# A fused convolution, state-space scan and expert layer: B read from SBUF instead of PSUM, one slot product on GpSimd, and another order at the end of the period

## The reference

```python
x = x + conv(_gn(x))                       # group norm, graph mixing of 64 nodes
t = tokens(x)
t = t + attn(_ln_t(t))                     # the scan below
t = t + ffn(_ln_t(t))                      # 8 experts, top 2 of them, gelu
```

```python
x_conv = silu(x_main @ W_conv + b_conv)
B_proj, C_proj = split(x_conv @ W_bc + b_bc)
dt = softplus(x_conv @ W_dt + b_dt)
h  = exp(dt_t[..., None] * A) * h + dt_t[..., None] * B_t[:, None, :] * x_t[..., None]
y_t = (h * C_t[:, None, :]).sum(-1)
y  = y * silu(x_gate)                      # then @ W_out + b_out
```

## Time and profile before

| what | us |
|---|---|
| three timed runs, median | 446.93 |
| lowest and highest of them | 444.72 and 447.65 |
| the profiled execution, its own time | 440.92 |
| its span in the profile | 439.2 |
| busy in the span: PE, DVE, ACT, POOL | 377.5, 338.7, 279.2, 247.9 |

### The profile page before, as it was taken

One profiled execution on the slowest core, in us unless ns is written; L12 is line 12 of the kernel. 1 busy time (PEld: TensorE's weight loads), 2 busy tenths in 40 slices (PEclk: granted clock), 3 DMA queues, 4 the chain that ended last, 5 costly groups with the idle time before them and its releaser, 6 DMA issues.

```text
span 439.2 us, 5613 instructions
## 1 busy us (share of the span) xinstructions
PE 377.5 (86%) x1785; PEld 207.6 (47%) x1785; DVE 338.7 (77%) x452; ACT 279.2 (64%) x450; POOL 247.9 (56%) x260
## 2 busy tenths in 40 slices
PE   0786779755699989998999899989988998998995
PEld 0673437212455346534653465355535544553652
DVE  3788347986499679987997799779987997996411
ACT  1002657843577887796779677986877785672472
POOL 9334004764259555875586558655873686387032
PEclk9997988969599999998999899999998999899999
DMA  8570079899999966997598769876988697000000
GB/s 211 163 146 1 0 175 222 222 227 221 226 217 219 225 167 150 228 208 175 137 223 198 175 143 226 187 175 151 220 185 203 141 225 164 1 1 0 13 0 12
DMA packets 22388, 67.91 MB, mean 155 GB/s; under 512 B 5052, under 2 KB 13400, under 8 KB 15448
## 3 DMA queue, kind: packets, MB, share of 16 engines
q1 hardware_dynamic: 21192, 66.73, 66.6%
q10 hardware_dynamic: 1168, 0.84, 0.8%
HBM read 62.32 MB, written 5.24 MB: 154 GB/s over the span
## 4 chain that ended last, share of the span: by engine, by line
PE 59%; DVE 16%; issue 7%; DMA 6%; ACT 5%; POOL 4%; SPq 0%; POOLq 0%; DVEq 0%; ACTq 0%
PE P L1119 11%; PE P L1105 7%; PE P L1135 6%; PE P L1059 5%; DMA av<-dt_scratch 5%; PE P L1106 5%; DVE hs L711 4%; PE P L991 4%; DVE P L704 4%; POOL hs L342 3%; PE P L1093 2%; PE P L1153 2%; PE P L1009 2%; PE P L1016 1%; PE P L1076 1%
## 5 line engine op out<-in xcount | busy, mean ns | idle before, releaser
L342 POOL TENSOR_TENSOR hs<-hs,Cs 128x1024 f32<-128x1024 f32 x64 | 151.7, 2371 | 83.5 <-DVE hs L711 83.5
L711 DVE TENSOR_TENSOR_SCAN hs<-av,P 128x1024 f32<-128x1024 f32 x64 | 146.3, 2287 | 3.2 <-DVE P L704 1.0
L704 DVE SCALAR_TENSOR_TENSOR P<-P,bbcol,ub 128x1024 f32<-128x1024 f32 x62 | 79.8, 1287 | 15.2 <-PE P L1026 12.2
L583 ACT ACTIVATE hb<-P,b1c 128x512 f32<-128x512 f32 x128 | 80.9, 684 | 16.0 <-PE P L1106 13.2
L545 ACT ACTIVATE av<-av,Aneg 128x510 f32<-128x510 f32 x92 | 61.1, 712 | 13.8 <-DMA av<-dt_scratch 13.8
L1119 PE MATMUL P<-hb,W2s 128*64 128x256 f32 x512 | 68.7, 391 | 0.0
L1105 PE MATMUL P<-X,W1H 128*128 128x512 f32 x128 | 56.1, 438 | 6.1 <-ACT av L545 6.1
L1135 PE MATMUL P<-W1H 128*128 128x512 f32 x164 | 56.0, 468 | 0.5 <-DVE rt L762 0.5
L1106 PE MATMUL P<-X,W1L 128*128 128x512 f32 x128 | 50.4, 394 | 0.0
L354 POOL TENSOR_TENSOR accs<-accs,mes 128x256 f32<-128x256 f32 x56 | 40.9, 731 | 12.2 <-DVE mes L796 7.3
L1119 PEld LDWEIGHTS P<-hb,W2s 128*64 128x64 f32 x512 | 31.3, 136 | 31.8 <-issue 22.1
(11 more groups left out here) (188 smaller groups left out, 483.1 us busy)
## 6 DMA issues: line engine op xcount, KB each, us to landing
ub<-u_scratch SPq DMA_DIRECT2D x31, 1024.0 KB, 11.6
av<-dt_scratch SPq DMA_DIRECT2D x23, 1024.0 KB, 7.4
dt_scratch<-dts SPq DMA_DIRECT2D x7, 256.0 KB, 2.8
u_scratch<-rl SPq DMA_DIRECT2D x7, 256.0 KB, 2.8
av<-in_L_conv_Wr SPq DMA_DIRECT2D x2, 576.0 KB, 6.6
av<-in_L_conv_Wl SPq DMA_DIRECT2D x2, 576.0 KB, 7.3
res<-in_x SPq DMA_DIRECT2D x4, 256.0 KB, 4.8
hb<-in_L_ffn_W SPq DMA_DIRECT2D x2, 512.0 KB, 5.5
```

The lines of the kernel that those rows point to most:

```text
L342: gp.tensor_tensor(hs[:, at, :, :], hs[:, at, :, :], rep(Cs[:, p, :], 1, 2), ALU.mult).then_inc(S["cm"], 1)
L583: a_.activation(hb[:, r % 4, :], P[:, (XA, XB)[r % 2], :], ACT.Gelu, bias=b1c[:, r:r + 1]).then_inc(S["gl"], 1)
L704: v.scalar_tensor_tensor(out=ring, in0=rep(P[:, BB, :], 1, 2), scalar=bbcol[:, 0:1], in1=ub[:, 2 * n:2 * n + 2, :], op0=ALU.add, op1=ALU.m ...
L711: v.tensor_tensor_scan(hs[:, (SLOTS * g + n) % RING].rearrange("p a t -> p (a t)"), av[:, 2 * n:2 * n + 2, :].rearrange("p a t -> p (a t)" ...
```

## The change

**B in SBUF.** ScalarE copies B from bank BB, with its bias, to a new buffer `Bs` of two halves (`act_b`), behind the first pair of gelus (in step 0 behind the last exponential). The product on VectorE becomes a tensor_tensor of `ub` and `Bs`, both in SBUF, still into `ring`; it waits for `bs` instead of `b_mm`. B's matmul stands before the first pair instead of at the end of the period.

**One product on GpSimd.** The product of slot 2 (POOLED) is made by GpSimd in place, ub = ub * Bs (`pool_product`), behind slot 1 and the low part; the scan of slot 2 reads `av` and `ub`, both in SBUF.

**The low part.** L754 leaves VectorE; GpSimd makes it (`pool_x2`) behind slot 1.

**The order.** The router's bias is added by VectorE (a new small tensor_tensor, `lgb`) instead of by TensorE, and its logits go to bank XC instead of YS. The spreads of dt for blocks 12 to 15 alternate between YS and XA. On TensorE the four sums stand together behind dt's projection; cenA and varA of step i+2 move between the spreads; the transpose of the router's weights stands behind pair 0 instead of pair 1, and what follows it is one pair earlier; the warming matmuls of a steady period go from 20 to 7. ScalarE follows with a new EXP_ORDER.

```diff
-EXP_ORDER = (0, 1, 2, 3, 4, 5, 6, 7, 8, 12, 9, 10, 13, 11, 14, 15)
+EXP_ORDER = (0, 1, 2, 3, 4, 5, 6, 7, 8, 9, 10, 12, 13, 11, 14, 15)
...
+        Bs = sb("Bs", [128, 2, T])
+        POOLED = 2
...
+        def pool_product(eng, g, p):
+
+            n = POOLED
+            eng.wait_ge(S["bs"], g + 1)
+            eng.wait_ge(S[f"u_in{n // 2}"], 16 * (g + 1))
+            at = ub[:, 2 * n:2 * n + 2, :]
+            gp.tensor_tensor(at, at, rep(Bs[:, p, :], 1, 2), ALU.mult).then_inc(S["pbm"], 1)
+
+        def pool_x2(eng, g):
+
+            eng.wait_ge(S["xh2"], g + 1)
+            eng.wait_ge(S["cm"], min(SLOTS * (g + 1) + 2, SLOTS * G))
+            since(eng, "acc", EXP * g)
+            gp.tensor_tensor(X2[64:128, :], xnt2[:, :], X2[0:64, :], ALU.subtract).then_inc(S["xl2"], 1)
+
         def pool_router(eng, g):
 
+            eng.wait_ge(S["xl2"], g + 1)
...
                 pool_slot(eng, i, p, 1)
+                if prev is not None:
+                    pool_x2(eng, prev)
+                    eng.wait_ge(S["xl2"], prev + 1)
+                pool_product(eng, i, p)
                 if prev is not None:
                     pool_router(eng, prev)
...
+        def act_b(eng, g, p):
+
+            eng.wait_ge(S["b_mm"], g + 1)
+            since(eng, "scan", SLOTS * (g - 1))
+            a_.activation(Bs[:, p, :], P[:, BB, :], ACT.Identity, bias=bbcol[:, 0:1]).then_inc(S["bs"], 1)
...
+            if n == POOLED:
+                eng.wait_ge(S["pbm"], g + 1)
+                src = ub[:, 2 * n:2 * n + 2, :]
             else:
...
-                v.scalar_tensor_tensor(out=ring, in0=rep(P[:, BB, :], 1, 2), scalar=bbcol[:, 0:1], in1=ub[:, 2 * n:2 * n + 2, :],
-                                       op0=ALU.add, op1=ALU.mult).then_inc(S["bm"], 1)
...
+                v.tensor_tensor(ring, u_of, rep(Bs[:, g % 2, :], 1, 2), ALU.mult).then_inc(S["bm"], 1)
...
-                                 ring.rearrange("p a t -> p (a t)"), 0.0, ALU.mult, ALU.add).then_inc(S["scan"], 1)
+                                 src.rearrange("p a t -> p (a t)"), 0.0, ALU.mult, ALU.add).then_inc(S["scan"], 1)
```

More of the change, by code:

```diff
@@ L627, in body @@
                     act_c(eng, nxt, q)
-                act_decay(eng, i, 9, 10, 13)
+                act_decay(eng, i, 12)
+                if nxt2 is not None:
+                    act_lnA1(eng, nxt2)
+                act_decay(eng, i, 13, 11)
+                if nxt2 is not None:
+                    act_lnA2(eng, nxt2)
                 if prev is not None:
                     act_router(eng, prev)
-                act_decay(eng, i, 11, 14, 15)
+                act_decay(eng, i, 14, 15)
+                if prev is None:
+                    act_b(eng, nxt, q)
                 if prev is not None:
@@ L635, in body @@
                         act_gelu(eng, prev, n)
-                        if n == 1:
+                        if n == 0 and nxt is not None:
+                            act_b(eng, nxt, q)
+                        if n == 0:
                             act_wt(eng, prev)
-                        if n in range(2, 6):
-                            act_wb(eng, prev, n - 2)
+                        if n in range(1, 5):
+                            act_wb(eng, prev, n - 1)
                 if nxt2 is not None:
@@ L661, in _ @@
             act_c(eng, 0, 0)
-            eng.wait_ge(S["b_mm"], 1)
-            a_.activation(B0, P[:, BB, :], ACT.Identity, bias=bbcol[:, 0:1]).then_inc(S["b0"], 1)
+            act_b(eng, 0, 0)
             act_lnA1(eng, 1)
@@ L682, in _ @@
                 act_gelu(eng, G - 1, n)
-                if n == 1:
+                if n == 0:
                     act_wt(eng, G - 1)
-                if n in range(2, 6):
-                    act_wb(eng, G - 1, n - 2)
+                if n in range(1, 5):
+                    act_wb(eng, G - 1, n - 1)
         ring = P[:, 0:2, :]
@@ L932, in body @@
                     dve_xn(eng, 1)
+                elif nxt is not None:
+                    dve_relu(eng, nxt)
                 if prev is not None:
                     dve_gate(eng, prev)
-                if i > 0 and nxt is not None:
-                    dve_relu(eng, nxt)
-                if prev is not None:
                     dve_t1(eng, prev, q)
@@ L1296, in body @@
                     pe_pair(eng, prev, 8)
-                pe_sum(eng, i, 0)
-                pe_sum(eng, i, 1)
                 if nxt2 is not None:
                     pe_dtz(eng, nxt2)
-                if nxt is not None:
-                    pe_b(eng, nxt)
-                pe_sum(eng, i, 2)
-                if i + 3 < G:
-                    pe_cenA(eng, i + 3)
-                if prev is not None:
-                    pe_warm(eng, 4, XB)
-                pe_sum(eng, i, 3)
+                for k in range(4):
+                    pe_sum(eng, i, k)
             for i in range(G):
@@ L1323, in _ @@
             pe_router(eng, G - 1)
-            eng.wait_ge(S["dd"], G)
             pe_warm(eng, 8)
             pe_pair(eng, G - 1, 0)
+            pe_wt(eng, G - 1)
             pe_warm(eng, 4)
-            pe_pair(eng, G - 1, 1)
-            pe_wt(eng, G - 1)
-            for n in range(2, 6):
+            for n in range(1, 5):
                 pe_pair(eng, G - 1, n)
-                pe_wb(eng, G - 1, n - 2)
-            for n in range(6, 9):
+                pe_wb(eng, G - 1, n - 1)
+            for n in range(5, 9):
                 pe_pair(eng, G - 1, n)
```

123 lines of the change are left out of this document (59 added, 64 removed).

## The result

The changed kernel takes 502.25 us in the median of 4 runs (497.95 to 506.07), the kernel before 445.83 beside it (444.19 to 447.65). The ratio is 1.123, with a 95% interval of 1.112 to 1.134: slower by 12%. I had predicted 498, in a range of 438 to 515. The profiled execution has a span of 502.6 against 439.2, so 63.4 are to be found.

A forecast was written before the change was run, and what follows sets the result against it. VectorE and TensorE were taken to share the bound. Under blocking, +48 for six periods, -1 for the last step, +8 at the start and 0 after the last scan gave +55 on 440.92, so 496; predicted 498, range 438 to 515.

The forecast's parts named there:

- The likeliest case: VectorE's two-SBUF-input instructions and GpSimd's SBUF reads block each other for whole instructions: 498 us likeliest, 465 to 515, chance 0.70.
- The price of blocking: VectorE's products beside GpSimd: each delayed between 0 and a whole GpSimd multiplication, 2.37 us; the blocking price was taken.
- two heaps: Product durations at L737: 1.2 us where GpSimd is idle, 2.5 to 3.0 where GpSimd began first.
- The period: Steady period under blocking, scan end to scan end: +7.1 to 50.8 us; six periods 305 instead of 256.7.
- 3 to 4: Slot 4: GpSimd, late from the router, multiplies slot 2 until 5.3 after scan 2; scan to scan 5.05 instead of 3.72.
- 4 to 5: Slot 5: the product waits behind GpSimd's multiplication after the experts; scan to scan 5.95 us instead of 4.28.
- The start: Up to slot 7 of step 1: +8 us; step 0 mostly hidden behind loads, step 1 has +8.5.
- the rule I gave for slot 3: Slot 3: with nothing between on VectorE, the product starts ahead of GpSimd; scan to scan 3.75 against 3.65.
- After the last scan: Tail of the kernel: GpSimd and VectorE hardly meet, so 0 us added.
- B's wait: Before slot 0's product: the 2.88 us wait per period for TensorE's B goes, turned into a wait for the port.
- no blocking: Rival, chance 0.22: VectorE's tensor_tensor runs freely beside GpSimd; 1.4 to 1.5 less for six periods, -9, 432 us.
- VectorE goes first: Variant of blocking: where GpSimd is behind, the product starts first, costing GpSimd 1.2, not VectorE 1.7; 454 to 475 us.

The follow-up runs named there:

- the one in which GpSimd is punctual: The changed kernel with slot 2's product back on VectorE, B still in SBUF: 518.51 us, ratio 1.166.

## Why the prediction was right, and where its sizes were off

The likeliest case (blocking, chance 0.70) came true, and the time lies 4 above the forecast. Step by step:

*The price of blocking.* Between 0 and a whole GpSimd multiplication I took the hold. Three runs stand behind it: 1,287 to 2,343 ns by B's place alone, back to 1,287 with B in PSUM, and 1,277 with fills on GpSimd. That L704's successor would fall into two heaps, 1.2 and 2.5 to 3.0, is half right: 26 of 54 lie there, 22 between 1.6 and 2.4, where only the end of a GpSimd instruction or a shorter one is in the way, and 6 reach 3.3 to 3.41, because a product that starts right behind GpSimd's start waits for all of it.

*The period.* Predicted 50.8 from scan end to scan end; the period to which the timelines above belong takes 50.35, from the end of slot 0's scan at 265.02 to the next at 315.37. Slot by slot, measured against predicted: 0 to 1, 7.07 and 7.25; 1 to 2, 10.62 and 10.95; 2 to 3, 3.78 and 3.75; 3 to 4, 4.09 and 5.05; 4 to 5, 7.20 and 5.95; then 5.86, 5.85 and 5.88 and each time 5.95. Two are off, and both come from what I overlooked at slot 2. I had counted the router's small steps only as victims on VectorE, never asked what the new scan does to GpSimd's. It holds L375 for 1.93. Hence the weights are late, TensorE idles and comes back at 1.2 GHz, and the experts let VectorE wait 2.48 (4 to 5 is longer). The other, 3 to 4, is shorter because I had GpSimd too late: its multiplication of slot 2 was to last until 5.3 after scan 2, but it starts at 284.81 and ends 4.46 after it, so slot 4's product waits only about 0.5. That the period is so near the forecast is in part luck, as -0.96 and +1.25 nearly cancel. The six steady periods take 297.6 (159.90 to 457.50) against 256.70: +40.9, where I had +47 for them (48, and 1 off for the last step). They are not all alike: in some, slot 1 takes 5.94 instead of 7.07, because the product starts 0.01 ahead of GpSimd's dts (317.76 and 317.77) and is free (1.22).

*The start.* I added 8 up to slot 7 of step 1; it is +15.4, 159.90 against 144.5. I had step 0 hidden behind its loads and +8.5 in step 1. It is the other way round: the end of slot 0's scan of step 1 comes at 115.67 against 100.27, already +15.4, and step 1 adds nothing, since the kernel before has a wait of its own there (18.5 from slot 1 to slot 2, against 10.9 after). VectorE's timeline of the changed kernel in step 0:

```profile
78.37 2.29 DVE L743 TENSOR_TENSOR_SCAN hs<-av,ub 128x1024 f32<-128x1024 f32 x1 [7.98 <-POOL ub L362]
...
92.46 3.41 DVE L737 TENSOR_TENSOR P<-ub,Bs 128x1024 f32<-128x1024 f32 x1
95.90 2.29 DVE L743 TENSOR_TENSOR_SCAN hs<-av,P 128x1024 f32<-128x1024 f32 x1
98.32 3.37 DVE L737 TENSOR_TENSOR P<-ub,Bs 128x1024 f32<-128x1024 f32 x1
```

and GpSimd's:

```profile
92.40 2.37 POOL L342 TENSOR_TENSOR hs<-hs,Cs 128x1024 f32<-128x1024 f32 x1 [3.49 <-DVE hs L743]
```

Of slot 3 I had written "here the product starts first, as VectorE has nothing between". Even with nothing between it is a matter of hundredths: GpSimd starts at 92.40, the product (here slot 5's) at 92.46, and all the products of slots 3 to 7 in step 0 take 3.3 to 3.4. In step 0 no slot has experts behind it, so the rule I gave for slot 3 would have made all of them free. That step failed. In the steady periods slot 3 came out as forecast (3.78 and 3.75), but because GpSimd is still in its router steps.

*After the last scan.* I had 0; it is 45.1 against 38.0, +7. Stretches of the changed kernel there:

```profile
457.50:470.00 12.50, 9.20 (x34) 5.88 (x35) 2.48 (x6) 1.84 (x5) 3.76 (x3) 0.73 0.04 10
470.00:476.00 6.00, 2.93 (x12) 1.77 (x10) 4.10 (x17) 2.78 (x4) 2.37 (x6) 0.89 0.02 3
476.00:482.00 6.00, 5.87 (x19) 3.61 (x20) 0.00 (x0) 1.75 (x3) 0.08 (x1) 0.54 0.00 0
482.00:502.60 20.60, 15.37 (x88) 8.51 (x87) 3.50 (x8) 9.98 (x16) 5.84 (x8) 0.99 0.03 7
```

TensorE is granted 0.73, 0.89 and 0.54 up to 482, and 0.99 over the rest; before, the whole stretch from 401.20 has 0.99. In the prediction's sum this is the term put at 0. The low part on GpSimd, 1.26 instead of 0.69, is on the path there too. Which of the two weighs more I didn't test.

*The gains.* B's wait went, as forecast, and was worth nothing: even with B in PSUM, taking most of it away brought 0. My rival "no blocking" with -9 had the right sign for the rest of the change: its order and the low part alone, with B in PSUM, gave -1.2%. Its other half, a product less for VectorE, costs 35 with B in PSUM. The rival "VectorE goes first" is there in part: some products of slot 1 start ahead of dts, and slot 3's, behind a router step of 0.25, holds L380. That such an order keeps the changed kernel 16 below the one in which GpSimd is punctual is my reading of the two timelines; no run shows it apart.

*The sum.* +15.4, +40.9 and +7.1 are the 63.4 of the two spans. The +55 predicted fell 8 short: 7 too little in the start, 6 too much in the periods, 7 too little in the tail.

## What to carry to other kernels

Before a VectorE operand is moved from PSUM to SBUF beside a busy GpSimd, count the SBUF inputs: with one of two in PSUM the products and scans ran beside GpSimd here without a loss, with both in SBUF each engine stood still behind the other for up to whole instructions, and the smallest instruction paid the most for its size. Two inputs are not the only case: VectorE's cast of 64x512, with one SBUF input, takes 0.42 free and in the kernel with B in PSUM 1.58 in the median, ending 0.29 behind GpSimd's multiplication (259.69 against 259.40). Where this can't be avoided, look not at the busy time but at what stands behind the held instruction: with B in PSUM a 32-column router step held by a scan cost 15 us, because TensorE waited for it, and a wait added on purpose won it back. And try the parts of a change apart, each on the base that will remain: the order was worth 0.8% by itself, the product on GpSimd was worth 16 with B in SBUF and cost 35 with B in PSUM.

## What the runs showed of the hardware that I had not expected

- Who starts first decides who pays, and hangs on hundredths. Both engines are released by the same scan end; GpSimd went first by 0.05 to 0.06 at 288.66 and 92.40. With B in SBUF alone the product of slot 3 started at 269.58, 0.04 ahead of GpSimd's 269.62; it took 1.23 and GpSimd's multiplication 3.42. The profile does not show what makes the product start 0.03 after a scan in one case and 0.12 in the other.
- A scan holds like any other VectorE instruction with two SBUF inputs: 0.24 became 2.16 on GpSimd. With one input in PSUM its 2,286 ns did not change, whatever GpSimd did. The scan can be held too: with slot 2's product of the kernel before written into ub, the scan of step 0 took 3.26 behind GpSimd's rl (L329), and the multiplication by C that came behind the scan 4.33.
- GpSimd's fills of the same tile, 0.95 to 0.97 for 1,024 columns, held nothing: the product took 1,277.
- A wait of 5.9 on TensorE was followed by 5.4 at 1.2 GHz. The price of a late operand on TensorE may thus be more than the wait in the table; no run measures the slow stretch apart.
